# Keys of the quantised attention made beside the product keys; context splits and context loads moved

## Chip, cores and metric

The kernel runs on one core of a Trainium2 chip, in one launch. The metric is device time in microseconds, the median over several runs. It is float32 throughout, with matrix products split in high and low parts where exactness asks for it.

## What is computed

Four layers act on x (2, 512, 512), each a cross attention on a context of 2 x 1024 tokens (512 features) and a feed-forward part, each added through a gate. Layer 0 has a linear attention and a ternary feed-forward part; layer 1 a masked softmax attention and a product-key part; layer 2 a softmax attention whose queries, weights and outputs are quantised, and routed experts; layer 3 a plain softmax attention and routed experts beside a shared one. Cut to what the change touches:

```python
# layer 0 attention (16 heads of 32, 64 features per head)
q_prime = relu(einsum('bhnd,fd->bhnf', q, Wqf)); k_prime = relu(einsum('bhnd,fd->bhnf', k, Wkf))
kv = einsum('bhnf,bhne->bhfe', k_prime, v)
out = einsum('bhmf,bhfe->bhme', q_prime, kv) / (einsum('bhmf,bhf->bhm', q_prime, k_prime.sum(2))[..., None] + 1e-8)
# layer 1 feed-forward: 4 heads, 2 sides of 128 keys
q = (x @ Wq).reshape(b, t, H, 2, DK)
s1, i1 = top_k(einsum('bthd,hkd->bthk', q1, keys[:, :, 0]), 8)   # and s2, i2
final_scores, pk_idx = top_k(s1[..., :, None] + s2[..., None, :], 8)
# layer 2 attention: only the query side depends on x
q = qdq(x) @ qdq(wq).T + bq
k, v = split(ctx @ wkv.T + bkv, 2)
o = softmax(q k^T / sqrt(32)) v;   out = qdq(o) @ qdq(wp).T + bp
```

## The kernel before

Each stage of each layer is a block of hand-written programs, one per engine (TensorE, VectorE, ScalarE, GpSimd, and SyncE for transfers), joined by semaphores. An engine takes its instructions in the order in which they stand; so each queue's order is the schedule.

**Linear attention** (`linear_attention_block`, L2015). A hardware loop runs over FG = 4 groups of heads. In one pass ScalarE drains 12 products, `i` from 0 to 11: four for the keys (L2238), two for the queries (L2241), two guests (L2246) and four for the mapped queries (L2248), which TensorE makes at L2180 into two PSUM slots; then TensorE makes the outputs (L2188). As a side work each pass splits a quarter of the context into a high and a low part for the later layers, in four steps c: ScalarE copies the high part (L2196), GpSimd subtracts (L2264), ScalarE issues the store to `ctx_parts` (L2200). There is one slot for it, `part[:, 2]`, so the copy of a step waits until the store of the step before has landed. The splits stand ahead of i = 0, 3, 6, 9, and the stores behind i = 2, 5, 8, 11:

```python
if i % 3 == 0: split_context(f, i // 3)
...
if i % 3 == 2: store_context(f, i // 3)
```

**Product keys** (`product_keys_block`, L1120), inside the layer 1 feed-forward block. TensorE makes queries (L1159), then similarities for 8 token tiles (L1169, 8 matmuls of 256 columns a tile). For each tile ScalarE copies them out (L1199 to L1202) and, two tiles later, adds score pairs (L398 in `ffn_block`); GpSimd makes small sums (L1222 and around); VectorE takes the largest values (L1245 to L1271) and the routing masks of two tiles before (L411, L418 of `ffn_block`). GpSimd also makes one large subtraction for the feed-forward weights (L380) at tile 2. TensorE is done with the similarities early and then has nothing to do until the block ends.

**Softmax attention** (`streamed_attention_block`, L1375, with `ContextLoads` and `AttentionParts`). Heads are worked in 8 sets of two. Work comes in items. A key item K (there are 16, two a set) is 12 matmuls of 128x512 (4 context chunks, and three terms high-high, high-low, low-high, L1626), a high part on ScalarE (L1758), a low part on VectorE (L1869) and a 512 KB store to `k_parts` (L1530), from which SyncE loads stacks (L1549). Q items make queries (L1617), V items values (L1638), X, W and N quantise x and wq and normalise. An opening works a written list of items; then each set runs score matmuls (L1675), row maxima (L1654, L1893), exponentials (L1788), value products (L1689), and sums of the exponentials: GpSimd adds tiles of 128x2048 (L1859), `DIRECT[n]` of the 8 addends of a set go to TensorE instead, which folds all (L1709). In the two attentions without a mask DIRECT is 0 but for set 6, so seven additions a set for GpSimd and six in set 6. Items of later sets stand between the score matmuls. The opening of layer 2 waits for `biases_loaded`, three loads, of which that of `bv` is issued last (L1370), behind one key weight, half of the context, two value weights and wq.

**Routed experts** (`routed_block`, L915). For each of I = 23 slots of tokens GpSimd gathers rows (L1058), TensorE turns and multiplies them (L972 to L1004) and GpSimd scatters the sums (L1066). In layer 2's block SyncE also loads the weights and context of layer 3's attention, 11 issues of half a MB, all at once after 5 slots: `sp.wait_ge(y_done, I // 4)`; `ahead(sp)`.

## Time and profile before

| | us |
|---|---|
| median of 3 runs | 3107.15 (3104.47 to 3112.45) |
| profiled execution | 3111.91 |
| its span | 3110.2 |
| TensorE busy | 2633.1 (85%) |
| VectorE busy | 1759.4 (57%) |
| ScalarE busy | 1196.3 (38%) |
| GpSimd busy | 958.0 (31%) |
| mean granted TensorE clock | 0.917 |

The stages, by the timeline: linear attention to 348, ternary feed-forward to 575, masked attention to 960, norm and product keys to 1095, their feed-forward part to 1553, quantised attention to 2030, routed experts to 2250, plain attention to 2660, last feed-forward part to 3110. TensorE is busy nearly everywhere; VectorE has its share in the product keys, GpSimd in the three softmax attentions, and transfers peak at the openings. The granted clock is full in most slices and falls where TensorE rests.

### The profile page before, as it was taken

What the parts mean: (1) busy time and instruction counts of PE and PEld (TensorE: products, weight loads), DVE (VectorE), ACT (ScalarE), POOL (GpSimd) and SP (SyncE); (2) the same over time, 40 slices, a digit from 0 to 9 for tenths busy, and PEclk for the clock granted to TensorE, in tenths of its full rate; (3) what the DMA queues carried; (4) which work ended last, traced back from release to release, by engine and by line L of the source; (5) the groups of instructions that cost most, each with busy time, mean ns of one, the idle gap of its engine ahead of it and who ended that gap; (6) DMA issues with size and microseconds to landing.
All of it is one profiled execution on the core that took longest, in us unless ns stands there. A gap on an engine that the chain in (4) does not pass through costs nothing. (4 is left out here: it accounts for less than half of the span.)

```text
span 3110.2 us, 36063 instructions
## 1 busy us (share of the span) xinstructions
PE 2633.1 (85%) x11399; PEld 1679.8 (54%) x11399; DVE 1759.4 (57%) x3263; ACT 1196.3 (38%) x2550; POOL 958.0 (31%) x440
## 2 busy tenths in 40 slices
PE   7888699888887279999969998748789998699898
PEld 3455388655423156555556563325575653477555
DVE  2433477567765989899367674512266773444222
ACT  0222122266652688787014455211125554222111
POOL 0221000056633110010015886032217883222122
PEclk9898799899988589999989998869999998799999
DMA  9554113566400010100064541075365530211822
GB/s 275 190 195 172 58 72 106 148 177 176 126 1 31 1 54 28 55 27 27 14 212 125 155 124 44 1 271 131 75 187 142 153 104 1 81 42 52 273 58 46
DMA packets 136826, 327.21 MB, mean 105 GB/s; under 512 B 18400, under 2 KB 21472, under 8 KB 133344
## 3 DMA queue, kind: packets, MB, share of 16 engines
q1 hardware_dynamic: 109472, 256.41, 26.7%
q0 software_dynamic: 12864, 29.06, 4.0%
q10 hardware_dynamic: 14336, 39.85, 3.9%
q8 instruction: 77, 1.26, 0.2%
q14 instruction: 77, 0.63, 0.1%
HBM read 230.94 MB, written 97.72 MB: 106 GB/s over the span
## 5 line engine op out<-in xcount | busy, mean ns | idle before, releaser
L1859 POOL TENSOR_TENSOR L_attn_total<-L_attn_total,L_attn_probs 128x2048 f32<-128x2048 f32 x109 | 499.4, 4582 | 39.8 <-ACT L_attn_probs L1788 30.1
L1893 DVE TENSOR_REDUCE L_attn_row_max<-L_attn_rows_ps 128x1 f32<-128x512 f32 x512 | 340.1, 685 | 150.9 <-PE L_attn_rows_ps L1654 145.9
L1788 ACT ACTIVATE L_attn_probs<-L_attn_s_ps 128x512 f32<-128x512 f32 x512 | 289.7, 601 | 277.2 <-PE L_attn_s_ps L1675 274.5
L516 PE MATMUL L_ffn_hidden<-L_ffn_x_high,L_ffn_up_high 128*128 128x512 f32 x688 | 296.4, 431 | 100.5 <-DVE L_ffn_routes L432 54.9
L398 ACT ACTIVATE L_ffn_sums<-sims 128x128 f32<-128x128 f32 x1024 | 315.5, 389 | 47.7 <-DVE L_ffn_routes L418 26.6
L1675 PE MATMUL L_attn_s_ps<-L_attn_q_stack,L_attn_k_stack 98*128 98x512 f32 (+1 forms) x768 | 312.6, 433 | 22.3 <-ACT L_attn_probs L1788 20.5
L516 PE MATMUL L_ffn_hidden<-L_ffn_x_low,L_ffn_up_high 128*128 128x512 f32 x688 | 273.6, 398 | 0.0
L1675 PEld LDWEIGHTS L_attn_s_ps<-L_attn_q_stack,L_attn_k_stack 98*128 98x128 f32 (+1 forms) x768 | 145.7, 194 | 163.2 <-ACT L_attn_probs L1788 80.5
L537 PE MATMUL L_ffn_y<-L_ffn_down_in,L_ffn_h 128*128 128x512 f32 x512 | 229.1, 593 | 0.4 <-DVE L_ffn_h L644 0.4
L1654 PE MATMUL L_attn_rows_ps<-L_attn_k_stack,L_attn_q_stack 96*128 96x512 f32 x512 | 217.1, 427 | 14.3 <-DMA L_attn_k_stack<-k_parts 8.4
L1788 ACT ACTIVATE L_attn_probs<-L_attn_s_ps,keep_mask 128x512 f32<-128x512 f32 x256 | 183.8, 782 | 84.8 <-DVE L_attn_s_ps L1905 84.5
L516 PEld LDWEIGHTS L_ffn_hidden<-L_ffn_x_high,L_ffn_up_high 128*128 128x128 f32 x688 | 132.7, 193 | 151.8 <-issue 81.0
L1626 PE MATMUL L_attn_product_ps<-L_attn_ctx,L_attn_wk 128*128 128x512 f32 x576 | 172.5, 420 | 47.4 <-DVE L_attn_ones L1919 26.4
L380 POOL TENSOR_TENSOR L_ffn_up_low<-L_ffn_up_in,L_ffn_up_high 128x512 fp32r<-128x512 f32 (+1 forms) x30 | 66.6, 2224 | 456.4 <-ACT L_ffn_up_high L374 456.4
L1689 PE MATMUL L_attn_s_ps<-L_attn_probs,L_attn_values 128*32 128x512 f32 x1536 | 199.9, 631 | 1.5 <-ACT L_attn_probs L1788 1.4
L1905 DVE TENSOR_SCALAR L_attn_s_ps<-L_attn_s_ps 128x512 f32<-128x512 f32 x256 | 163.4, 688 | 60.5 <-PE L_attn_s_ps L1675 58.9
L1638 PE MATMUL L_attn_product_ps<-L_attn_wv,L_attn_ctx 128*128 128x256 f32 x1152 | 169.0, 288 | 14.4 <-DMA L_attn_wv<-L_attn_kv_parts 5.1
L1638 PEld LDWEIGHTS L_attn_product_ps<-L_attn_wv,L_attn_ctx 128*128 128x128 f32 x1152 | 163.5, 195 | 27.6 <-DVEq L1917 6.5
L516 PE MATMUL L_ffn_hidden<-L_ffn_x_high,L_ffn_up_low 128*128 128x512 f32 x432 | 173.2, 401 | 0.0
L1859 POOL TENSOR_TENSOR L_attn_total<-L_attn_probs 128x2048 f32<-128x2048 f32 x21 | 96.1, 4577 | 248.2 <-ACT L_attn_probs L1788 248.2
L1626 PEld LDWEIGHTS L_attn_product_ps<-L_attn_ctx,L_attn_wk 128*128 128x128 f32 x576 | 116.2, 203 | 77.6 <-DVE L_attn_ones L1919 27.7
L516 PEld LDWEIGHTS L_ffn_hidden<-L_ffn_x_low,L_ffn_up_high 128*128 128x128 f32 x688 | 133.2, 194 | 36.4 <-issue 10.5
(300 smaller groups left out, 4451.0 us busy)
## 6 DMA issues: line engine op xcount, KB each, us to landing
L_attn_k_stack<-k_parts SPq DMA_DIRECT2D x144, 256.0 KB, 4.8
k_parts<-L_attn_stage SPq DMA_DIRECT2D x48, 512.0 KB, 2.7
L_attn_q_stack<-q_parts SPq DMA_DIRECT2D x72, 256.0 KB, 6.3
L_attn_abs_in<-in_L_ffn_w SPq DMA_DIRECT2D x12, 1024.0 KB, 11.5
L_attn_kv_parts<-L_attn_part ACTq DMA_DIRECT2D x12, 1024.0 KB, 4.8
L_attn_wk<-L_attn_kv_parts SPq DMA_DIRECT2D x24, 512.0 KB, 4.3
L_attn_ctx<-ctx_parts SPq DMA_DIRECT2D x24, 512.0 KB, 10.9
L_attn_wv<-L_attn_kv_parts SPq DMA_DIRECT2D x24, 512.0 KB, 9.3
```

Source lines behind the costliest of these rows:

```text
L398: last = nc.scalar.activation(sums[:, h, a * NK:(a + 1) * NK], sims[:, t, h, KEY_ROWS:KEY_ROWS + NK], ACT.Identity, bias=sims[:, t, h, bas ...
L516: last = nc.tensor.matmul(hidden_ps[0:m, b, side, :], w[:, i, e0:e0 + m], x_parts[xp][:, i, h * HALF:(h + 1) * HALF], start=(q == 0), stop ...
L537: last = nc.tensor.matmul(y_ps[:, t % YB, :], h_parts[hp][0:m, s, c, t * P:(t + 1) * P], down_parts[wp][0:m, s, c, :], start=(q == 0), sto ...
L1626: last = nc.tensor.matmul(to, wk[:, w, c * P:(c + 1) * P], ctx[:, i, x, c, :], start=(c == 0 and (w, x) == TERMS[0]), stop=(c == DC - 1 an ...
L1638: last = nc.tensor.matmul(to[:, c // 2 * PAIR * P:(c // 2 + 1) * PAIR * P], ctx[:, i, x, d, at:at + P], wv[:, half, w, d % 2 * PAIR * P:(d ...
L1654: nc.tensor.matmul(rows_ps[:, r % R_SLOTS, :], q_stack[0:FOLD, n % Q_SLOTS, h, q * P:(q + 1) * P], k_stack[0:FOLD, n % 2, h, i * HALF:(i + ...
L1675: nc.tensor.matmul(s_ps[:, v % S_SLOTS, :], k_stack[0:depth, n % 2, h, kt * P:(kt + 1) * P], q_stack[0:depth, n % Q_SLOTS, h, :], start=Tr ...
L1689: last = nc.tensor.matmul(o_ps[HD * h:HD * (h + 1), :], values[:, n // PAIR % V_SLOTS, kt, at:at + HD], probs[:, g % P_SLOTS, h, :], start ...
L1788: nc.scalar.activation(probs[:, g % P_SLOTS, h, :], s_ps[:, v % S_SLOTS, :], ACT.Exp, **kinds).then_inc(exp_done, 1)
L1859: nc.gpsimd.tensor_tensor(total[:], first, probs[:, g % P_SLOTS], ALU.add).then_inc(added, 1)
L1893: nc.vector.tensor_reduce(row_max[:, hq, i:i + 1], rows_ps[:, r % R_SLOTS, :], AX_X, ALU.max, negate=True).then_inc(max_done, 1)
L1905: nc.vector.tensor_scalar(scores, scores, BOUND / SCALE, -BOUND / SCALE, ALU.min, ALU.max).then_inc(clipped, 1)
```

## The change

There are four parts, and the results are the same.

1. The 16 key items of layer 2's attention leave it. Their matmuls are in the product-key block, behind the similarities of tiles 2 to 7, by the table `AHEAD_AT`. A product goes into one of 4 PSUM slots that the queries used; ScalarE writes the high part and the raw product (L1226 and L1228 of the changed kernel) to one of 4 stage slots, GpSimd subtracts one from the other, SyncE stores 512 KB. The weights (4 x 512 KB) and the first of four context pieces (2 MB each, two buffers) are loaded in the norm block ahead. SyncE waits in the feed-forward block until the four slots are stored (`settle`), before the down weights are loaded.
2. Layer 2's attention has no K items. `bv` is loaded fourth, and the first key stacks before the second context half. The 32 row matmuls of set 0 ride on items V02 to Q11 rather than K10 to Q11. DIRECT is 1 for every set, so GpSimd makes six additions a set instead of seven, and TensorE folds one addend more.
3. Linear attention: splits at i = 1, 6, 8 and behind the loop's products; stores one product behind each, the last behind its split.
4. Layer 3's loads are ten pieces, issued at y_done of 1, 3, 5, ... 19, rather than all at 5.

```diff
 # product_keys_block
+    AHEAD_AT = {2: (0, 1), 3: (2, 3, 4), 4: (5, 6, 7), 5: (8, 9, 10), 6: (11, 12, 13), 7: (14, 15)}
 # SyncE
+                sp.wait_ge(q_psum, 2 * H)
+                ahead.load_piece(env, sp, 1)
+                for m in range(ahead.COUNT):
+                    ahead.store(env, sp, m)
+                    piece = m // DC + 2
+                    if m % DC == DC - 1 and piece < ahead.PIECES:
+                        sp.wait_ge(ahead.psum, m + 1)
+                        ahead.load_piece(env, sp, piece)
 # TensorE
+                def key_product(m):
...
+                    if m >= 4:
+                        pe.wait_ge(ahead.raw, m - 3)
+                    for c in range(DC):
+                        for w, x in TERMS:
+                            last = nc.tensor.matmul(q_ps[:, m % 4, :], ahead.wk[:, f, w, c * P:(c + 1) * P],
...
                 for t in range(2, TILES):
                     similarities(t)
+                    for m in AHEAD_AT[t]:
+                        key_product(m)
 # ScalarE
+                def key_parts(m):
...
+                    if m >= ahead.SLOTS:
+                        act.wait_ge(ahead.stored[s], 16 * (m // ahead.SLOTS))
+                    if m == 2:
+                        first["up_taken"](act)
+                    nc.scalar.activation(ahead.stage[s][:, 0], q_ps[:, m % 4, :], ACT.Identity, bias=bias).then_inc(
+                        ahead.high, 1)
+                    nc.scalar.activation(ahead.stage[s][:, 1].bitcast(F32), q_ps[:, m % 4, :], ACT.Identity,
+                                         bias=bias).then_inc(ahead.raw, 1)
 # GpSimd
+                def key_low(m):
...
+                    nc.gpsimd.tensor_tensor(stage[:, 1], stage[:, 1].bitcast(F32), stage[:, 0].bitcast(F32),
+                                            ALU.subtract).then_inc(ahead.low, 1)
 # streamed_attention_block
-    DIRECT = {n: int(n == SETS - 2) if less_max_rows else 3 if n == SETS - 2 else 2 for n in range(SETS - 1)}
+    made = parts.keys_made
+    DIRECT = {n: int(made or n == SETS - 2) if less_max_rows else 3 if n == SETS - 2 else 2 for n in range(SETS - 1)}
-        order = ("N0 K00 X0 X1 N2 V00 V01 X2 X3 W0 W1 N4 Q00 K01 X4 X5 W2 W3 N6 Q01 V02 V03 X6 X7 K10 K11 "
-                 "Q02 Q03 Q10 Q11 T0 Q12 Q13")
+        order = ("N0 X0 X1 N2 W0 W1 X2 X3 N4 Q00 V00 V01 X4 X5 W2 W3 N6 Q01 V02 V03 X6 X7 Q02 Q03 Q10 Q11 T0 Q12 Q13")
 # linear_attention_block
+    SPLIT_AT = {1: 0, K_PARTS + Q_PARTS: 1, K_PARTS + Q_PARTS + GUESTS: 2}
-                        if i % 3 == 0:
-                            split_context(f, i // 3)
+                        if i in SPLIT_AT:
+                            split_context(f, SPLIT_AT[i])
...
-                        if i % 3 == 2:
-                            store_context(f, i // 3)
+                        if i - 1 in SPLIT_AT:
+                            store_context(f, SPLIT_AT[i - 1])
...
+                    split_context(f, DC - 1)
+                    store_context(f, DC - 1)
 # routed_block
-                if ahead:
-                    sp.wait_ge(y_done, I // 4)
-                    ahead(sp)
+                pieces = ahead() if ahead else []
+                for k, piece in enumerate(pieces):
+                    sp.wait_ge(y_done, 1 + k * (I - 2) // len(pieces))
+                    piece(sp)
```

ScalarE, linear attention, from the drain of product 8 on (its own first row below is the drain, L2248; L2196 the context copy, L2200 its store, L2211 a split of later weights). Before:

```order
L2248 ACTIVATE L_attn_qf<-L_attn_proj_ps 128x512
L2199 REGISTER_ALU
L2200 ISA
L2200 DMA ctx_parts<-L_attn_part 256x1x512
L2195 ISA
L2196 ISA
L2196 COPY L_attn_part<-L_attn_ctxT 128x512
L2235 REGISTER_ALU
L2248 ACTIVATE L_attn_qf<-L_attn_proj_ps 128x512
```

and in the changed kernel (drain L2375, copy L2323, store L2327, later weights L2338):

```order
L2323 COPY L_attn_part<-L_attn_ctxT 128x512
L2362 REGISTER_ALU
L2375 ACTIVATE L_attn_qf<-L_attn_proj_ps 128x512
L2362 REGISTER_ALU
L2375 ACTIVATE L_attn_qf<-L_attn_proj_ps 128x512
L2326 REGISTER_ALU
L2327 ISA
L2327 DMA ctx_parts<-L_attn_part 256x1x512
L2336 REGISTER_ALU
L2337 REGISTER_ALU
L2338 CAST L_attn_part<-L_attn_later_raw 128x2x512
L2362 REGISTER_ALU
```

The copy that stood between the drains of products 8 and 9 stands ahead of that of 8; the next one stands behind the last drain of the pass.

SyncE, start of layer 2's attention, before:

```order
L1366 DMA L_attn_bq<-in_L_attn_bq 128x4
L1366 DMA L_attn_bk<-in_L_attn_bk 128x4
L1310 DMA L_attn_wk<-L_attn_kv_parts 128x1024
L1302 DMA L_attn_ctx<-ctx_parts 128x2x512 x4
L1314 DMA L_attn_wv<-L_attn_kv_parts 128x1024 x2
L1369 DMA L_attn_wq_raw<-wq_scratch 128x4x512
L1370 DMA L_attn_bv<-in_L_attn_bv 128x512
L1302 DMA L_attn_ctx<-ctx_parts 128x2x512 x4
```

and in the changed kernel (L1664 loads key stacks):

```order
L1473 DMA L_attn_bq<-in_L_attn_bq 128x4
L1473 DMA L_attn_bk<-in_L_attn_bk 128x4
L1475 DMA L_attn_wq_raw<-wq_scratch 128x4x512
L1476 DMA L_attn_bv<-in_L_attn_bv 128x512
L1370 DMA L_attn_wv<-L_attn_kv_parts 128x1024 x2
L1358 DMA L_attn_ctx<-ctx_parts 128x2x512 x4
L1664 DMA L_attn_k_stack<-k_parts 32x4x512 x6
L1358 DMA L_attn_ctx<-ctx_parts 128x2x512 x4
```

The load of `bv` stands behind 1 MB of wq rather than behind that and seven half-MB loads.

ScalarE, product keys, from the pair sums of the third tile on (L398; L1199 or L1244 copies similarities), before:

```order
L398 ACTIVATE L_ffn_sums<-sims 128x128 x16
L374 CAST L_ffn_up_high<-L_ffn_up_in 128x2048
L1199 COPY L_ffn_full<-L_ffn_sims_ps 128x1024
L1201 COPY sims<-L_ffn_full 128x4x32
L1202 COPY sims<-L_ffn_full 128x4x128
L398 ACTIVATE L_ffn_sums<-sims 128x128 x16
```

and in the changed kernel (names of the slots differ, `L_ffn_up_in` is one of them):

```order
L398 ACTIVATE L_ffn_sums<-sims 128x128 x16
L374 CAST L_ffn_up_high<-L_ffn_up_in 128x2048
L1226 ACTIVATE ahead_stage<-L_ffn_q_ps,ahead_bk 128x512
L1228 ACTIVATE ahead_stage<-L_ffn_q_ps,ahead_bk 128x512
L1226 ACTIVATE ahead_stage<-L_ffn_q_ps,ahead_bk 128x512
L1228 ACTIVATE ahead_stage<-L_ffn_q_ps,ahead_bk 128x512
L1244 COPY L_ffn_full<-L_ffn_sims_ps 128x1024
L1246 COPY sims<-L_ffn_full 128x4x32
L1247 COPY sims<-L_ffn_full 128x4x128
L398 ACTIVATE L_ffn_sums<-sims 128x128 x16
L1226 ACTIVATE L_ffn_up_in<-L_ffn_q_ps,ahead_bk 128x512
L1228 ACTIVATE L_ffn_up_in<-L_ffn_q_ps,ahead_bk 128x512
```

Between two tiles stand two or three pairs of activations on key products.

## Rows read from the trace of the kernel before

**Rows 1.** Timeline, linear attention: start, us, operation, idle before and its releaser.
```profile
130.22 1.22 PE L2180 MATMUL L_attn_proj_ps<-L_attn_qT,L_attn_wqf 128*128 128x512 f32 x1 [7.12 <-ACT L_attn_qf L2248]
...
189.87 0.62 ACT L2196 CAST L_attn_part<-L_attn_ctxT 128x512 fp32r x1 [5.80 <-DMA ctx_parts<-L_attn_part]
...
191.04 1.22 PE L2180 MATMUL L_attn_proj_ps<-L_attn_qT,L_attn_wqf 128*128 128x512 f32 x1 [5.79 <-ACT L_attn_qf L2248]
...
307.93 0.70 PE L2180 MATMUL L_attn_proj_ps<-L_attn_qT,L_attn_wqf 128*128 128x512 f32 x1 [2.78 <-ACT L_attn_qf L2248]
```

**Rows 2.** Timeline, TensorE, then VectorE over one tile of the product keys.
```profile
996.78 1.89 PE L1169 MATMUL L_ffn_sims_ps<-L_ffn_keys,L_ffn_qT 128*128 128x256 f32 x8
...
1060.97 1.64 DVE L1245 MAX8 L_ffn_best<-L_ffn_full 128x8 f32<-128x128 f32 x8
...
1067.63 0.75 DVE L411 SCALAR_TENSOR_TENSOR L_ffn_sums<-L_ffn_sums,bar 128x512 f32<-128x512 f32 x1
...
1071.63 0.29 DVE L1245 MAX8 L_ffn_best<-L_ffn_full 128x8 f32<-128x128 f32 x1
```

**Rows 3.** Windows, that tile: us, busy of PE, PEld, DVE, ACT, POOL, PEclk, DMA.
```profile
1060.97:1071.63 10.66, 0.00 (x0) 0.00 (x0) 9.97 (x37) 6.70 (x21) 1.05 (x4) 0.50 0.00 1
```

**Rows 4.** Timeline, one GpSimd operation and the VectorE operation that began under it.
```profile
1020.87 4.52 POOL L380 TENSOR_TENSOR L_ffn_up_low<-L_ffn_up_in,L_ffn_up_high 128x2048 fp32r<-128x2048 f32 x1 [3.75 <-ACT L_ffn_up_high L374]
...
1020.90 5.04 DVE L411 SCALAR_TENSOR_TENSOR L_ffn_sums<-L_ffn_sums,bar 128x512 f32<-128x512 f32 x1
```

**Rows 5.** Timeline, TensorE and ScalarE, prices in the quantised attention.
```profile
1616.72 0.86 PE L1626 MATMUL L_attn_product_ps<-L_attn_ctx,L_attn_wk 128*128 128x512 f32 x3
...
1617.42 0.40 PE L1654 MATMUL L_attn_rows_ps<-L_attn_k_stack,L_attn_q_stack 96*128 96x512 f32 x1
...
1749.11 0.68 ACT L1758 ACTIVATE L_attn_stage<-L_attn_product_ps,L_attn_bk 128x512 fp32r<-128x512 f32 x1
...
1890.98 0.63 PE L1654 MATMUL L_attn_rows_ps<-L_attn_k_stack,L_attn_q_stack 96*128 96x512 f32 x1
...
1891.41 0.63 PE L1675 MATMUL L_attn_s_ps<-L_attn_q_stack,L_attn_k_stack 98*128 98x512 f32 x1
```

**Rows 6.** The page, DMA issues: KB each, us from issue to landing.
```profile
k_parts<-L_attn_stage SPq DMA_DIRECT2D x48, 512.0 KB, 2.7
```

**Rows 7.** Timeline, start of the quantised attention's opening.
```profile
1561.93 1.03 SPq L1370 DMA_DIRECT2D L_attn_bv<-in_L_attn_bv  x1
...
1573.43 0.30 ACT L1802 ACTIVATE L_attn_sd<-tile_meanvar,eps_ln 128x8 f32<-128x8 f32 x1 [11.91 <-DMA L_attn_bv<-in_L_attn_bv]
```

**Rows 8.** Windows, that opening, columns as before.
```profile
1573.40:1652.80 79.40, 64.44 (x302) 52.21 (x302) 64.44 (x105) 14.41 (x26) 5.43 (x4) 0.89 0.60 177
```

**Rows 9.** Timeline, GpSimd and TensorE, the sets of the quantised attention.
```profile
1721.79 0.80 PE L1654 MATMUL L_attn_rows_ps<-L_attn_k_stack,L_attn_q_stack 96*128 96x512 f32 x1 [4.39 <-DMA L_attn_k_stack<-k_parts]
...
1778.58 4.59 POOL L1859 TENSOR_TENSOR L_attn_total<-L_attn_probs 128x2048 f32<-128x2048 f32 x1 [2.26 <-ACT L_attn_probs L1788]
...
1793.19 1.29 POOL L1838 TENSOR_TENSOR L_attn_heads<-L_attn_spare 128x512 f32<-128x512 f32 x1
...
1887.67 1.93 PE L1709 MATMUL L_attn_product_ps<-L_attn_total,L_attn_ones 128*32 128x512 f32 x8 [2.02 <-POOL L_attn_total L1859]
```

**Rows 10.** Windows, sets 0 to 5 together, set 4 alone, set 6 alone.
```profile
1660.14:1891.04 230.90, 222.77 (x1232) 140.02 (x1232) 161.57 (x249) 119.93 (x216) 198.78 (x47) 0.98 0.48 131
1815.52:1853.01 37.49, 36.91 (x211) 23.56 (x210) 27.52 (x43) 19.98 (x37) 33.33 (x8) 1.00 0.41 106
1891.04:1925.95 34.91, 29.70 (x128) 11.51 (x126) 14.83 (x23) 17.52 (x33) 28.48 (x7) 0.79 0.00 1
```

**Rows 11.** Timeline, routed experts: the last load of a burst, and a wait.
```profile
2122.60 5.49 SPq L1302 DMA_DIRECT2D L_attn_ctx<-ctx_parts  x4
...
2129.97 0.47 PE L972 MATMUL L_ffn_x_ps<-ident,L_ffn_xg 128*128 128x128 f32 x1 [8.05 <-DMA L_ffn_xg<-L_ffn_x_slots]
```

More of the change, by code:

```diff
@@ L1212, in _ @@
             def _(pool):
+                def key_low(m):
+                    stage = ahead.stage[m % ahead.SLOTS]
+                    pool.wait_ge(ahead.high, m + 1)
+                    pool.wait_ge(ahead.raw, m + 1)
+                    nc.gpsimd.tensor_tensor(stage[:, 1], stage[:, 1].bitcast(F32), stage[:, 0].bitcast(F32),
+                                            ALU.subtract).then_inc(ahead.low, 1)
                 for t in range(TILES):
@@ L1223, in _ @@
                         first["gpsimd"](pool)
+                    for m in AHEAD_AT.get(t, ()):
+                        key_low(m)
             @block.vector
@@ L1320, in load_first, with pieces_ahead @@
         self.load_value_weights(sp, 0)
+    def pieces_ahead(self, env):
+        self.ahead = True
+        halves = [[lambda sp, i=i, c=c: self.load_context(env, sp, 0, i, c) for c in range(DC)] for i in range(CTX // HALF)]
+        return [lambda sp: self.load_key_weights(sp, 0), *halves[0], lambda sp: self.load_value_weights(sp, 0), *halves[1]]
     def load_ahead(self, env, sp):
@@ L1325, in load_ahead, with __init__, place, load_weights @@
         self.load_half(env, sp, 0, 1)
+class KeysAhead:
+    PIECES, SLOTS = BATCH * CTX // HALF, 4
+    def __init__(self, env, kv_parts, bias):
+        env.prefix = "L2_keys_ahead"
+        self.kv_parts, self.bias = kv_parts, bias
+        self.weights_loaded = env.sem("weights_loaded")
+        self.ctx_loaded = [env.sem(f"ctx_loaded{s}") for s in range(2)]
+        self.psum, self.high, self.raw, self.low = env.sem("psum"), env.sem("high"), env.sem("raw"), env.sem("low")
+        self.stored = [env.sem(f"stored{s}") for s in range(self.SLOTS)]
+        self.COUNT = self.PIECES * DC
+    def place(self, env, first, stage_at, ctx_at, local):
+        nc = env.nc
+        self.wk = local.enter_context(nc.sbuf_tensor("ahead_wk", [P, DC, 2, DC * P], F32R))
+        self.bk = local.enter_context(nc.sbuf_tensor("ahead_bk", [P, DC], F32))
+        early = nc.alloc_sbuf_tensor_at("ahead_stage", [P, 2, 2, HALF], F32R, offset=stage_at)
+        late = first["up_in"].rearrange("p (s h n) -> p s h n", s=2, h=2).bitcast(F32R)
+        self.stage = [early[:, 0], early[:, 1], late[:, 0], late[:, 1]]
+        second = nc.alloc_sbuf_tensor_at("ahead_ctx", [P, 2, DC, HALF], F32R, offset=ctx_at)
+        self.ctx = [[up.rearrange("p (c n) -> p c n", c=DC) for up in first["up_next"]], [second[:, 0], second[:, 1]]]
+    def load_weights(self, sp):
+        sp.dma_start(self.bk[:], self.bias).then_inc(self.weights_loaded, 16)
+        for f in range(DC):
+            sp.dma_start(self.wk[:, f].bitcast(F32), self.kv_parts[f, :, 0].bitcast(F32)).then_inc(self.weights_loaded, 16)
+    def load_piece(self, env, sp, piece):
+        for part in range(2):
+            sp.dma_start(self.ctx[piece % 2][part].bitcast(F32), env.ctx_parts[piece, :, part].bitcast(F32)).then_inc(
+                self.ctx_loaded[piece % 2], 16)
+    def store(self, env, sp, m):
+        piece, f = m // DC, m % DC
+        halves = CTX // HALF
+        sp.wait_ge(self.low, m + 1)
+        sp.dma_start(env.k_parts[piece // halves * DC + f, piece % halves].bitcast(F32),
+                     self.stage[m % self.SLOTS].bitcast(F32)).then_inc(self.stored[m % self.SLOTS], 16)
+    def settle(self, sp):
+        for s in range(self.SLOTS):
+            sp.wait_ge(self.stored[s], 16 * (self.COUNT // self.SLOTS))
@@ L1398, in streamed_attention_block @@
     CHUNK_AT = {u: (item, c) for item, units in enumerate(((0, 1, 3, 4), (8, 9, 11, 12), (14, 15, 16, 17), (20, 21, 23, 24)))
-                for c, u in enumerate(units)}
-    DONE_AT = {max(u for u in CHUNK_AT if CHUNK_AT[u][0] == i) + 1: i for i in range(4)}
+                for c, u in enumerate(units) if not made or item % 2 == 0}
+    DONE_AT = {max(u for u in CHUNK_AT if CHUNK_AT[u][0] == i) + 1: i for i in range(0, 4, 1 + made)}
     SUMS_AT = 7 if less_max_rows else PV_AT
@@ L1544, in stack_keys @@
                 def stack_keys(n, i):
-                    stored(sp, ("K", n, i))
+                    if not made:
+                        stored(sp, ("K", n, i))
                     if n >= 2:
@@ L1568, in _ @@
                 ready = []
+                if made:
+                    loads.load_value_weights(sp, 0)
+                    loads.load_half(env, sp, 0, 0)
+                    for i in range(KH):
+                        stack_keys(0, i)
+                    loads.load_half(env, sp, 0, 1)
                 for item in OPENING:
@@ L2611, in attention_layer @@
                         key_mask_block(env, name, keep_mask)
-                    parts = AttentionParts(env, name, loads, work)
+                    parts = AttentionParts(env, name, loads, work, kinds.get("keys_made", False))
                     streamed_attention_block(env, name, heads_out, parts, keep_mask, env.io["wo"], early, quantised)
```

88 lines of the change are left out of this document (63 added, 25 removed).

## The prediction

> **What bounds the kernel now.** I read first the page's busy slices, to see which engine limits which stage, then the timeline of each stage that the change touches, for the waits that end last there, and then windows over one period of each, for how much room the other engines have.
>
> In the **linear attention** the chain runs through ScalarE's drains. The second mapped product waits for a PSUM slot: 7.12 us of idle TensorE in the first pass, 5.79 in the second, 2.78 in the last (the third, not shown, like the second). Just ahead of each the copy of a context chunk has stood 5.80 us for the store before it, and it takes 0.62 itself [rows 1]. So a side work's landing is on the path, four times.
>
> In the **product keys** VectorE is the bound: one tile takes from 1060.97 to 1071.63, 10.66 us [rows 2], of which VectorE is busy 9.97, ScalarE 6.70, GpSimd 1.05 and TensorE not at all, at a granted clock of 0.50, the lower level [rows 3].
>
> In the **quantised attention** the opening loses 11.91 us to the load of `bv`, issued at 1561.93 behind all others [rows 7], and from there to the first scores at 1652.8 TensorE and VectorE are each busy 64.4 of 79.4 us [rows 8]. In the sets both TensorE and GpSimd are near their limit: TensorE 222.8 of 230.9 us over six sets, and of set 4's 37.49 us GpSimd 33.3, TensorE 36.9 [rows 10].
>
> In the **routed experts** SyncE issues the last four of 11 loads at 2122.60, and TensorE then stands 8.05 us for gathered rows [rows 11].
>
> **The sum**, against the profiled execution of 3111.9 us, which is 4.8 above the median of the runs shown.
>
> *Linear attention: -24.* The copy leaves the place between products 8 and 9. Waits of TensorE there are 7.12 + 5.79 + 5.79 + 2.78 = 21.5, and four copies of 0.62 add 2.5 to the chain [rows 1]. In their new places, the copy at i = 8 falls in the time in which ScalarE waits for TensorE's key maps, that at i = 1 waits for the last of the pass before, issued under the outputs; the last stands behind all drains. None adds to the chain unless a store lands later than there. Low end -27 (the clock of the last matmuls gains too), high end -15, if a third of it comes back as a wait at another step.
>
> *Product keys: +12.* Added to each of tiles 3 to 6: 36 matmuls on TensorE, six activations on ScalarE, three subtractions on GpSimd (tiles 2 and 7: two thirds). TensorE: 36 x 0.233 (three of this shape from 1616.72 to 1617.42 [rows 5]) is 8.4, and the 8 similarities 1.9 [rows 2], so 10.3 against 10.66: just hidden, since the engine is idle there. ScalarE: 6.70 + 6 x 0.68 [rows 3, 5] = 10.8: also about even, and tiles 2 and 7 have fewer. GpSimd: three of 1.29 [rows 9] are room enough. But its operations hit VectorE. While GpSimd held one of 4.52 us, a VectorE operation that began 0.03 us later took 5.04 [rows 4] and not its usual 0.75 [rows 2]. So the bound engine pays for each of 16 subtractions: 0 if none meets an operation of two inputs, and 16 x 1.29 = 20.6 if each is paid in full. Operations of that sort are the seven masks and routes of a tile (L411, L418), at 0.75 each [rows 2] some 5 us, and the small ones at L1265 to L1267, some 1.3: about 0.6 of the tile, so 16 x 1.29 x 0.6 = 12 is taken. The Trainium skill, SBUF — State Buffer, "SBUF: two separate sides", says that the port pair that the two share is an exclusive lock held for a whole instruction; by it each collision costs the rest of GpSimd's operation, and the part would be 20 rather than 12 if VectorE always needed the lock. The row of 5.04 us agrees. The loads (10 MB with the weights) run where the transfers stand still [rows 3]. The ring of four slots: product 2.8, two activations 1.4, subtraction 1.3, store 2.7 [rows 5, 6, 9], about 8 to 12 us around, against 3.5 us an item: that is 14 us for four, so it doesn't bind. `settle` finds the last store a few us old; the down weights behind it are needed only after the first up products.
>
> *Opening: -20.* `bv` lands before it is needed, -11 (11.91 less what is left of a shorter queue). Four key items leave the 79.4 us: 48 matmuls x 0.233 = 11.2 us of TensorE and four parts of 0.7 on VectorE; with TensorE 81% busy I take -9. Ends: -14 (items move into gaps) and -24.
>
> *Sets: -22.* A set loses one GpSimd addition (4.59), 24 matmuls (5.6) on TensorE, and gets 8 short ones (0.9). GpSimd's cycle would be 37.5 - 4.6 = 32.9, TensorE's 36.9 - 4.7 = 32.2. Against that, the one set with six additions and no key items, set 6, took 34.91 with a clock of 0.79 [rows 10], because TensorE waits for GpSimd at the fold (2.02 us) [rows 9] and then runs at the lower level: 0.43 us from 1890.98 to 1891.41 [rows 5]. I take 34.9 for each of the six: 6 x 34.9 = 209.4, against 230.9, which also holds the 4.39 us in which a key stack was late [rows 9]. Ends: -33 (6 x 32.9) and -5 (only the stall goes).
>
> *Loads of layer 3: -6* of the 8.05 us [rows 11], since one piece at a time lets the gathers through; ends 0 and -10. Everything behind is as before.
>
> Sum: -24 + 12 - 20 - 22 - 6 = **-60**: the profiled execution would be 3052, the median **3047**.
>
> **Rivals.**
>
> *A. TensorE stays at the lower level in the product keys.* It stood at 0.50 there [rows 3], and a wait between products could hold it. Then 36 x 0.43 + 3.8 = 19.3 us a tile for four tiles and 14.1 for two: 4 x 8.6 + 2 x 3.5 = +42 and not +12, so 3077. Against: with 97% of the tile filled it never rests.
>
> *B. Collisions in full and no gain from spreading.* +20.6 for +12, 0 for -6: 3062. The Trainium skill, DMA: Bandwidth & Descriptors, "Queues, rings and completion order", says that each engine takes packets from its queues in turn; spread loads would then still halve the gathers as they pass, only at ten places. The row at 2129.97 can't tell a burst from a stream.
>
> *C. The sets keep their cycle.* Set 6's clock says how: with less work TensorE rests, slows, and scores come at the old pace. Only the stall goes: -5 for -22, so 3064.
>
> *D. Slower: the slot ring.* If a round of PSUM, ScalarE, GpSimd and store takes R, each item takes R/4, and ScalarE, waiting for `stored`, holds back the similarity copies and pair sums that VectorE lives on. The six tiles take 64 us; the change turns slower where 16 R / 4 is over 64 + 12 + 60 - that is R above 34. With 40: 160 - 64 = +96 for +12, 3131. For it: ScalarE is at 10.8 of 10.7, and GpSimd queues behind VectorE in the same collisions. Against: four stages of 8 us.
>
> *E. The change does not do what it says*: GpSimd's one addition less and the keys' absence are undone by waits on values and queries, so that the time stays within 0.3% (9 us, about what a measurement of this kernel tells from no change).
>
> **How the numbers follow.** The forecast has 0.62, A 0.12, B 0.09, C 0.12, D 0.03, E 0.02. The best ends together give -27 + 0 - 24 - 33 - 10 = -94, the worst -15 + 20.6 - 14 - 5 - 0 = -13. The range leaves the tails, D and E, out: 3020 to 3080, which holds A, B and C. Faster 0.95, same 0.02, slower 0.03.
>
> **What would show it.** In the linear attention no TensorE wait at the mapped products over 1 us, and 24 us less at its end. In the product keys TensorE at full clock at tiles 3 to 6 with a period of about 12.5 us on VectorE, some of its operations above 1.5 us; a period of 19 with a pitch of 0.43 is A, activations waiting for `stored` are D. In the opening no wait for `bv` and the first score 20 us sooner. In the sets a period near 35 and PEclk of 0.8 to 0.9; near 33 is better than forecast, near 37 is C. In the routed experts no wait of 8 us for gathered rows. The forecast is wrong if VectorE waits for ScalarE in the product keys, or if a wait for key stacks comes up in the sets.

## The result, and the profile after

| | us |
|---|---|
| before, median | 3105.81 (3103.9 to 3112.45) |
| changed, median | 3058.24 (3056.32 to 3059.69) |
| ratio | 0.9843, 95% interval 0.9826 to 0.986 |
| changed, profiled execution, span | 3057.55, 3055.8 |
| TensorE, VectorE, ScalarE, GpSimd busy | 2624.9, 1756.1, 1205.2, 951.3 |
| mean granted TensorE clock | 0.933 |

The change is faster by 48 us. Between the two profiled executions it is 54.4. Anchors that both traces have, such as the first turn behind the linear attention or the first matmul of a stage, put these 54.4 us in their places:

| part | forecast | between the traces |
|---|---|---|
| linear attention | -24 | -27.0 (turn at 325.04, now 298.04) |
| up to the queries of the product keys | 0 | -2.2 (976.93, now 947.77) |
| product keys | +12 | +12.1 (118.3 to 130.4 from first query to first hidden product) |
| opening of layer 2 | -20 | -10.9 (98.1 to 87.2 from the first load to the first score) |
| sets 0 to 5 | -22 | -13.5 (230.9 to 217.4) |
| routed experts | -6 | -9.3 (244.1 to 234.8 from the first turn to the first product of layer 3) |
| all else | 0 | -3.6 |

**Linear attention.** In the timeline of the changed kernel (start, duration, operation, idle before and its releaser) the copy of the third split still waits for the store before it, but now ahead of the drain of product 8, where ScalarE has nothing to drain before 173.26; and TensorE goes from the mapped products to the outputs with a short wait only:

```profile
161.01 0.62 ACT L2323 CAST L_attn_part<-L_attn_ctxT 128x512 fp32r x1 [3.81 <-DMA ctx_parts<-L_attn_part]
...
177.33 1.10 PE L2315 MATMUL L_attn_o_ps<-L_attn_kv,L_attn_qf 128*128 128x66 f32 x8 [1.43 <-ACT L_attn_qf L2375]
...
231.10 1.10 PE L2315 MATMUL L_attn_o_ps<-L_attn_kv,L_attn_qf 128*128 128x66 f32 x8 [1.44 <-ACT L_attn_qf L2375]
```

The pass is 52.6 us from 124.78 to 177.33, where it was about 60; nothing answers to the waits of 7.12, 5.79 and 2.78 us [rows 1]. Two windows over the whole loop, before and changed (us, busy of PE, PEld, DVE, ACT, POOL, PEclk, DMA share, GB/s):

```profile
78.00:325.04 247.04, 204.71 (x774) 125.56 (x772) 103.25 (x237) 49.88 (x76) 48.34 (x28) 0.87 0.54 186
...
78.00:298.04 220.04, 195.16 (x773) 119.79 (x771) 99.50 (x237) 49.89 (x76) 48.34 (x28) 0.92 0.58 206
```

Of the 27.0 us, 17.5 are idle time of TensorE (42.3 to 24.9) and 9.5 are busy time: the same matmuls run at a granted clock of 0.92 instead of 0.87.

**Product keys.** One tile on VectorE, with the operation at L1321 (0.87 us in a tile of the kernel before, where it is L1265), and below it GpSimd's two rows of subtractions in that tile:

```profile
1040.18 1.64 DVE L1301 MAX8 L_ffn_best<-L_ffn_full 128x8 f32<-128x128 f32 x8
...
1044.67 2.81 DVE L1321 SCALAR_TENSOR_TENSOR L_ffn_reach<-L_ffn_pairs,bar 128x64 f32<-128x64 f32 x4
...
1053.21 0.28 DVE L1301 MAX8 L_ffn_best<-L_ffn_full 128x8 f32<-128x128 f32 x1
```

```profile
1043.23 1.29 POOL L1264 TENSOR_TENSOR L_ffn_up_in<-L_ffn_up_in 128x512 fp32r<-128x512 f32 x1 [0.23 <-ACT L_ffn_up_in L1228]
...
1044.48 2.53 POOL L1264 TENSOR_TENSOR ahead_stage<-ahead_stage 128x512 fp32r<-128x512 f32 x2
```

The tile takes 13.03 us and was 10.66 [rows 2]. The subtractions lie from 1043.23 to 1047.01. VectorE's four small operations at L1321 begin under the second one and take 2.81 us, 1.94 more; another 0.36 is a longer gap ahead of L1305. The seven masks and routes have their usual times, since GpSimd is done when they begin. The window over the tile, in the columns above:

```profile
1040.18:1053.21 13.03, 5.45 (x23) 3.84 (x21) 11.98 (x37) 10.16 (x27) 4.82 (x7) 0.86 0.31 122
```

ScalarE is at 10.16, and TensorE's clock 0.86 rather than 0.50 [rows 3]. (Some of its matmul records are missing there.) The waits listed for ScalarE in these tiles are for VectorE's masks, none for a store of the ring.

**Opening.** ScalarE's first operation waits 0.33 us for `bv` and not 11.91 [rows 7]; but TensorE stands 4.46 us for a row maximum that VectorE can only take behind its last normalisation:

```profile
1545.27 0.30 ACT L1927 ACTIVATE L_attn_sd<-tile_meanvar,eps_ln 128x8 f32<-128x8 f32 x1 [0.33 <-DMA L_attn_bv<-in_L_attn_bv]
...
1586.45 1.39 PE L1779 MATMUL L_attn_rows_ps<-L_attn_k_stack,L_attn_q_stack 96*128 96x512 f32 x2 [4.46 <-DVE L_attn_row_max L2019]
```

The window from the first normalisation to the first score is 80.0 us, as long as before (79.4), though TensorE's work fell from 64.4 to 57.0 [rows 8]. VectorE's fell by 2.3.

```profile
1545.27:1625.28 80.01, 56.98 (x266) 46.26 (x266) 62.16 (x101) 11.97 (x22) 5.37 (x4) 0.79 0.63 181
```

**Sets.** A set is 32 units of one score and one row matmul each; a value or key item is laid between them in four pieces, the chunks. The windows are sets 0 to 5 together, then sets 1, 3 and 5, and 4 us within set 3:

```profile
1632.65:1850.01 217.36, 207.02 (x1137) 114.39 (x1136) 152.39 (x237) 112.87 (x205) 170.84 (x42) 0.98 0.39 98
...
1667.95:1703.92 35.97, 34.12 (x195) 18.88 (x193) 25.95 (x41) 18.94 (x35) 28.69 (x7) 1.00 0.65 183
...
1741.37:1778.75 37.38, 35.52 (x194) 20.14 (x193) 25.91 (x41) 18.75 (x35) 28.64 (x8) 0.95 0.37 93
...
1816.15:1850.01 33.86, 31.93 (x171) 15.82 (x169) 25.12 (x40) 18.50 (x35) 28.69 (x8) 1.00 0.33 87
...
1749.00:1753.00 4.00, 4.00 (x19) 3.61 (x18) 1.73 (x3) 1.19 (x2) 3.86 (x2) 0.57 0.53 131
```

GpSimd's busy time in the six sets fell from 198.8 to 170.8, TensorE's from 222.8 to 207.0 [rows 10], yet set 3 takes 37.4 us where it took 36.9. Within it the clock is 0.57 from 1749 to 1753. Rows of TensorE, the first from set 1, the others from set 3 up to that drop:

```profile
1674.78 0.50 PE L1779 MATMUL L_attn_rows_ps<-L_attn_k_stack,L_attn_q_stack 96*128 96x512 f32 x1 [0.98 <-DVE L_attn_row_max L2019]
...
1746.49 0.50 PE L1779 MATMUL L_attn_rows_ps<-L_attn_k_stack,L_attn_q_stack 96*128 96x512 f32 x1 [0.50 <-DVE L_attn_row_max L2019]
...
1748.19 0.50 PE L1779 MATMUL L_attn_rows_ps<-L_attn_k_stack,L_attn_q_stack 96*128 96x512 f32 x1 [0.96 <-DVE L_attn_row_max L2019]
...
1749.59 0.63 PE L1779 MATMUL L_attn_rows_ps<-L_attn_k_stack,L_attn_q_stack 96*128 96x512 f32 x1
...
1750.02 1.48 PE L1763 MATMUL L_attn_product_ps<-L_attn_wv,L_attn_ctx 128*128 128x256 f32 x6
```

Units without a chunk come one after the other here; each has a score and a row matmul, 0.47 us, and a maximum of 0.685 us on VectorE, for which there are two PSUM slots. TensorE waits 0.50 and 0.96 us for a maximum, and then a row matmul takes 0.63 and six value matmuls 1.48 rather than 0.87 us: the lower level. But the wait does not settle it: sets 1 and 5 have the same waits (0.48 and 0.98) and stay at 1.00, while sets 2, 3 and 4 fall to 0.95 each. That difference costs 1.4 us (36.0 against 37.4), and what decides it is not shown.

The trace of before shows little of this. The list of waits (us in total, times, longest), over sets 2 to 4 before and then in the changed kernel, has:

```profile
PEld L_attn_rows_ps L1654 <- DVE L_attn_row_max L1893: 4.7, 12, 0.5
...
PEld L_attn_rows_ps L1779 <- DVE L_attn_row_max L2019: 19.1, 36, 1.4
PE L_attn_rows_ps L1779 <- DVE L_attn_row_max L2019: 4.9, 9, 1.0
```

Before, no matmul of these three sets is listed as waiting for a maximum, only 12 weight loads.

**Routed experts.** SyncE's loads come over some 120 us (four of them from 2058.32 in the first row), and the longest wait for gathered rows in that time is one of 3.10 us, against 8.05 [rows 11]:

```profile
2058.32 40.85 SPq L1358 DMA_DIRECT2D L_attn_ctx<-ctx_parts  x4
...
2126.39 0.66 PE L978 MATMUL L_ffn_x_ps<-ident,L_ffn_xg 128*128 128x128 f32 x4 [1.09 <-DMA L_ffn_xg<-L_ffn_x_slots]
...
2154.84 0.66 PE L978 MATMUL L_ffn_x_ps<-ident,L_ffn_xg 128*128 128x128 f32 x4 [3.10 <-DMA L_ffn_xg<-L_ffn_x_slots]
```

### The profile page after: what moved, and what is told of

The parts are those of the page before. It is cut to its first block and busy times, and to the rows that moved or that the text cites. A ratio compares the mean times of both kernels' runs of the same rounds, so it can differ in the third digit from the quotient of the medians.

```text
span 3055.8 us, 36190 instructions
## 1 busy us (share of the span) xinstructions
PE 2624.9 (86%) x11447; PEld 1668.5 (55%) x11447; DVE 1756.1 (57%) x3247; ACT 1205.2 (39%) x2566; POOL 951.3 (31%) x450
## 5 line engine op out<-in xcount | busy, mean ns | idle before, releaser
L1985 POOL TENSOR_TENSOR L_attn_total<-L_attn_total,L_attn_probs 128x2048 f32<-128x2048 f32 x103 | 471.5, 4577 | 29.7 <-ACT L_attn_probs L1913 19.7
L398 ACT ACTIVATE L_ffn_sums<-sims 128x128 f32<-128x128 f32 x1024 | 315.4, 389 | 41.2 <-DVE L_ffn_routes L418 25.8
L1779 PE MATMUL L_attn_rows_ps<-L_attn_k_stack,L_attn_q_stack 96*128 96x512 f32 x512 | 223.4, 440 | 24.4 <-DVE L_attn_row_max L2019 17.6
L1779 PEld LDWEIGHTS L_attn_rows_ps<-L_attn_k_stack,L_attn_q_stack 96*128 96x128 f32 x512 | 99.2, 194 | 90.4 <-DVE L_attn_row_max L2019 71.7
L542 PEld LDWEIGHTS L_ffn_y<-L_ffn_down_in,L_ffn_h 128*128 128x128 f32 x512 | 93.5, 191 | 98.9 <-issue 98.9
```

Source lines behind the costliest of these rows:

```text
L398: last = nc.scalar.activation(sums[:, h, a * NK:(a + 1) * NK], sims[:, t, h, KEY_ROWS:KEY_ROWS + NK], ACT.Identity, bias=sims[:, t, h, bas ...
L542: last = nc.tensor.matmul(y_ps[:, t % YB, :], h_parts[hp][0:m, s, c, t * P:(t + 1) * P], down_parts[wp][0:m, s, c, :], start=(q == 0), sto ...
L1779: nc.tensor.matmul(rows_ps[:, r % R_SLOTS, :], q_stack[0:FOLD, n % Q_SLOTS, h, q * P:(q + 1) * P], k_stack[0:FOLD, n % 2, h, i * HALF:(i + ...
L1985: nc.gpsimd.tensor_tensor(total[:], first, probs[:, g % P_SLOTS], ALU.add).then_inc(added, 1)
```

## The experiments

All are measured beside runs of the kernel before on the same chip; a kernel's runs lie within 3 to 19 us of each other, so that the place of a difference is read from the profiled execution and its sign from the interval.

**The subtractions.** The changed kernel without `key_low`, so that the low parts of these keys stay the raw products:

```diff
-                    nc.gpsimd.tensor_tensor(stage[:, 1], stage[:, 1].bitcast(F32), stage[:, 0].bitcast(F32),
-                                            ALU.subtract).then_inc(ahead.low, 1)
...
-        sp.wait_ge(self.low, m + 1)
+        sp.wait_ge(self.high, m + 1)
+        sp.wait_ge(self.raw, m + 1)
```

> The changed kernel without the 16 subtractions of GpSimd in the product keys; the low part of the early keys is left as the raw product, so the keys of layer 2 are not the reference's. Theory (a GpSimd operation on 128x512 holds back VectorE by about 0.8 us each, and nothing else lengthened a tile): the period of a tile on VectorE goes from 13.05 us in the changed kernel back to 10.7, and the kernel from 3058 to about 3046, -12. Rival (ScalarE's six more activations of 0.68 us a tile lengthen it, since similarity copies and pair sums stand behind them): the period stays at 13 and the time at 3058.

Measured: 3053.2 us, ratio 0.9828 (0.9806 to 0.985); the profiled execution 3048.3. A tile on VectorE, and the window over it:

```profile
1023.35 1.64 DVE L1292 MAX8 L_ffn_best<-L_ffn_full 128x8 f32<-128x128 f32 x8
...
1033.95 1.64 DVE L1292 MAX8 L_ffn_best<-L_ffn_full 128x8 f32<-128x128 f32 x8
```

```profile
1023.35:1033.95 10.60, 10.60 (x49) 8.86 (x48) 9.92 (x36) 10.18 (x27) 1.05 (x4) 1.00 0.65 263
```

The period is 10.60 us, and the stage 118.8 us, against 130.4 with the subtractions and 118.3 before. ScalarE's 10.18 us fit into the tile, and TensorE is busy all of it at full clock. So 16 subtractions cost 11.6 us, 0.73 each, and 192 matmuls, 32 activations, the transfers and the slots cost 0.5, no more than the stage varies between runs of one code (130.4 to 131.6). The rival falls. The whole kernel gained less than the stage, 5 us in the medians and 9.3 in the profiled executions: sets 1 and 5 have the drop of the clock in this execution (37.4 and 35.3 us for 36.0 and 33.9), which takes back 2.9.

**The order of the value chunks.** In layer 2 only:

```diff
-    CHUNK_AT = {u: (item, c) for item, units in enumerate(((0, 1, 3, 4), (8, 9, 11, 12), (14, 15, 16, 17), (20, 21, 23, 24)))
+    CHUNK_AT = {u: (item, c) for item, units in enumerate(((0, 2, 4, 6), (), (9, 13, 17, 21), ()) if made else
```

> The changed kernel with the two value items of a set at units 0, 2, 4, 6 and 9, 13, 17, 21 instead of 0, 1, 3, 4 and 14, 15, 16, 17, in layer 2 alone. Theory (row maxima on VectorE, 0.685 us each, pace the units that carry no product chunk, and TensorE rests there, drops to the lower clock level and loses the rest): the wait of about 1 us and the stretch at half clock behind it go, the period of sets 2 to 4 falls from 37.4 to about 35, and the six periods together from 217 to about 205, so 3046. Rival (GpSimd or ScalarE sets the cycle, or the clock drops whatever the order): within 3 us of 3058.

Measured: 3059.8 us, ratio 0.9846 (0.9823 to 0.9868), no different from the change, as the rival had it. Sets 2 to 4 take 35.9 us each; set 3, and a wait in set 1:

```profile
1743.79:1779.69 35.90, 34.40 (x194) 19.11 (x193) 25.54 (x41) 18.31 (x35) 28.64 (x7) 1.00 0.38 97
...
1688.08 0.50 PE L1780 MATMUL L_attn_rows_ps<-L_attn_k_stack,L_attn_q_stack 96*128 96x512 f32 x1 [2.28 <-DMA L_attn_k_stack<-k_parts]
```

The clock is 1.00 in sets 2 to 5, and the waits of 0.5 and 1.0 us are gone there, so the drop of the clock is a matter of where the chunkless units stand, worth 1.5 us a set. But 35.9 is also what set 1 of the changed kernel took at full clock (36.0): beyond the clock the new places gave nothing. Set 1 takes 38.8 for 36.0, with a wait of 2.28 us for a key stack and a clock of 0.96, which took 2.8 back: the six sets are 215.2 us for 217.4, not 205. The theory holds for the clock alone.

**Seven additions.**

```diff
-    DIRECT = {n: int(made or n == SETS - 2) if less_max_rows else 3 if n == SETS - 2 else 2 for n in range(SETS - 1)}
+    DIRECT = {n: int(n == SETS - 2) if less_max_rows else 3 if n == SETS - 2 else 2 for n in range(SETS - 1)}
```

> The changed kernel with DIRECT as before: seven additions on GpSimd in sets 0 to 5, and eight matmuls fewer on TensorE at the fold. Theory (VectorE and TensorE pace a set, GpSimd has 6.8 us of waiting in each): a set gets 0 to 1 us shorter or stays, 3052 to 3060. Rival (GpSimd's additions set the cycle, so that the sixth addition's removal is where the gain of the sets comes from): a set gets up to 4.6 us longer where GpSimd's wait was smaller, 3065 to 3080.

Measured: 3068.8 us, ratio 0.9882 (0.9858 to 0.9906). Sets 2 and 5:

```profile
1703.55:1741.15 37.60, 34.75 (x186) 20.01 (x185) 25.92 (x41) 18.93 (x35) 33.26 (x8) 0.95 0.36 92
...
1816.32:1855.00 38.68, 33.77 (x162) 17.28 (x161) 24.95 (x40) 18.43 (x34) 33.16 (x9) 0.90 0.29 76
```

Sets 2 to 4 take 37.6 us, 0.2 more than with six additions. TensorE has eight matmuls fewer, 0.9 us, and waits 0.97 us at each fold for GpSimd: the one pays for the other. Set 5, whose window has one value item instead of two, goes from 33.9 to 38.7: there GpSimd, busy 33.2 us, is the bound again. So the removed addition paid 4.8 us in one set and 1.3 in the other five together, at the pace that VectorE sets. A set of 32.9 us, as in the run with short maxima below, would have no room for 33.3 us of additions.

**Rows behind the last normalisation.**

```diff
-        order = ("... N6 Q01 V02 V03 X6 X7 Q02 Q03 Q10 Q11 T0 Q12 Q13")
+        order = ("... N6 Q01 X6 X7 V02 V03 Q02 Q03 Q10 Q11 T0 Q12 Q13")
```

> The changed kernel with X6 and X7 ahead of V02 and V03 in the opening of layer 2, so that no row matmul waits for VectorE's last normalisation. Theory (the opening is a chain on VectorE: normalisations, then 32 row maxima of set 0; TensorE's 4.46 us of waiting and its half clock behind it are covered): the first score moves by 3 us at most, 3055 to 3060. Rival (that wait and the lower clock that follows cost what the key items' removal should have saved): 3050 or less.

Measured: 3064.7 us, ratio 0.9871 (0.9844 to 0.9897), the profiled execution 3054.4; the interval overlaps that of the change. From the first normalisation to the first score it takes 81.5 us, for 80.0. The wait of 4.46 us is gone and nothing is won: it was covered. Set 1:

```profile
1668.70:1706.12 37.42, 35.53 (x194) 20.20 (x193) 25.95 (x41) 18.96 (x35) 28.67 (x8) 0.95 0.63 176
```

It had 36.0 in the changed kernel, and set 5 takes 35.3 for 33.9: whether a set has the drop of the clock can differ where its code is the same.

**Half of each maximum.** Maxima over 256 of 512 scores:

```diff
-                    nc.vector.tensor_reduce(row_max[:, hq, i:i + 1], rows_ps[:, r % R_SLOTS, :], AX_X, ALU.max,
+                    wide = SEQ // 2 if made else SEQ
+                    nc.vector.tensor_reduce(row_max[:, hq, i:i + 1], rows_ps[:, r % R_SLOTS, 0:wide], AX_X, ALU.max,
```

> The changed kernel with the row maxima of layer 2 taken over 256 of each 512 scores, so that VectorE's reduction is about half as long (some 0.4 instead of 0.685 us). The other half of the scores is left out of the maximum that is subtracted before the exponential, nothing else. Theory (VectorE's maxima pace the units without a product chunk, and the second half of the opening): sets 2 to 4 fall from 37.4 us to 32 to 34 each, no wait of TensorE for a maximum remains, and the time from the first normalisation to the first score falls from 80 us by 6 to 10; in all 3058 to about 3030. Rival (GpSimd's additions or ScalarE's exponentials set the period): sets within 1 us of 37.4, opening unchanged, 3053 to 3060.

Measured: 3037.9 us, ratio 0.9766 (0.975 to 0.9782). One maximum, then the windows of set 2 and of the opening:

```profile
1730.02 0.36 DVE L2020 TENSOR_REDUCE L_attn_row_max<-L_attn_rows_ps 128x1 f32<-128x256 f32 x1
```

```profile
1695.86:1728.78 32.92, 32.20 (x194) 18.93 (x193) 18.08 (x40) 18.18 (x35) 28.75 (x7) 1.00 0.43 106
...
1547.16:1623.16 76.00, 54.09 (x265) 45.35 (x266) 52.37 (x101) 11.97 (x22) 5.38 (x4) 0.81 0.67 190
```

Sets 1 to 4 take 32.9 us each, with TensorE busy 32.2: 4.5 less than sets 2 to 4 had, of which 1.4 is the clock, and 3.1 less than set 1, which had been at full clock. That is the 32.2 that the prediction had worked out for TensorE; the rest is one wait of 0.7 us a set for a maximum, which the expectation had as gone. GpSimd still waits 3.6 us in each. VectorE's maxima are what held the sets. In the opening 10 us less work on VectorE gave 4.0, less than the 6 to 10 expected: VectorE is not alone in that chain. This kernel is the fastest here, 20 us below the change. It subtracts a number that need not be the row's maximum, which is exact in exact arithmetic and safe while the other half's scores are not higher by more than an exponential can hold.

**The matmuls put back.** Row matmuls issued four times where key chunks stood:

```diff
-                            row(of, r)
+                            row(of, r, 4 if made and n + AHEAD < SETS and u in (8, 9, 11, 12, 20, 21, 23, 24) else 1)
```

> The changed kernel with the row matmul issued four times instead of once at units 8, 9, 11, 12, 20, 21, 23, 24 of sets 0 to 5 of layer 2, where the key chunks stood; 24 matmuls a set are added, 5.6 us of TensorE, as many as the change took out. Theory (the key chunks stood in time that TensorE has to wait for VectorE anyway, and kept its clock up): the periods of sets 2 to 4 stay at 36.5 to 38, 3055 to 3065. Rival (TensorE's own work sets the period and 5.6 us less of it was a gain given back elsewhere): each set gets 4 to 5.6 us longer, 3080 or more.

Measured: 3073.0 us, ratio 0.9872 (0.9846 to 0.9899). Set 3:

```profile
1748.64:1787.64 39.00, 38.22 (x219) 23.80 (x218) 26.26 (x41) 18.97 (x35) 28.77 (x8) 1.00 0.36 89
```

A set takes 39.0 us: 1.6 more than the changed kernel's 37.4, and 3.0 more than a set of it at full clock (set 1, 36.0). The clock is 1.00. Neither expectation holds: of 5.6 us of matmuls 2.6 are hidden behind VectorE, and 1.4 come back as clock, so that in sets 2 to 4 TensorE's relief was worth 1.6 us and not 5.6. A repeated row matmul also delays its own maximum, which a key chunk did not; the 1.6 is thus an upper end.

**The splits alone**, on the kernel before (GpSimd's subtractions follow them; not shown):

```diff
-                        if i % 3 == 0:
-                            split_context(f, i // 3)
+                        if i in SPLIT_AT:
+                            split_context(f, SPLIT_AT[i])
...
-                        if i % 3 == 2:
-                            store_context(f, i // 3)
+                        if i - 1 in SPLIT_AT:
+                            store_context(f, SPLIT_AT[i - 1])
```

> The kernel before with the context splits of the linear attention moved, alone. Theory (each pass has one landing of a store and one copy between products 8 and 9 on the chain): -27 us, as between the two traces at the end of the linear attention, 3079 against 3106. Rival (part of the 27 comes from elsewhere, as the transfers of the changed norm block): less than 22.

Measured: 3084.0 us, ratio 0.9917 (0.989 to 0.9945). The first turn is at 298.24 against 325.04 before, -26.8, and the span 3082.3, -27.9. The loop to that turn:

```profile
78.00:298.24 220.24, 195.31 (x774) 119.58 (x772) 99.48 (x237) 49.85 (x76) 48.36 (x28) 0.92 0.58 206
```

The whole gain is the splits', that of the clock too.

**`bv` first alone**, on the kernel before (its later load goes):

```diff
+        if self.early_bias:
+            sp.dma_start(self.bv[:], io["bv"].partition_broadcast(P)).then_inc(self.biases_loaded, 16)
         if not self.loads.ahead:
             self.loads.load_first(env, sp)
```

> The kernel before with the load of bv in layer 2 ahead of the key weight, the context and the value weights, alone; the keys stay where they are. Theory (the opening gained only by the earlier load, the key items' removal nothing): the first normalisation starts some 12 us sooner but TensorE's first key item still waits for its context, 16 us after the block's start, so that X0 and what is behind it on TensorE stand behind it: -6 to -11. Rival (VectorE's chain is held by the key item ahead of X0 and X1 on TensorE): under 3 us of gain.

Measured: 3100.1 us, ratio 0.9974 (0.9959 to 0.9989). From the first load to the first score 91.8 us, for 98.1: -6.3. The new wait, on TensorE and, behind it, on VectorE:

```profile
1565.15 5.05 PE L1630 MATMUL L_attn_product_ps<-L_attn_ctx,L_attn_wk 128*128 128x512 f32 x12 [16.99 <-DMA L_attn_ctx<-ctx_parts]
...
1571.10 0.75 DVE L1873 SCALAR_TENSOR_TENSOR L_attn_stage<-L_attn_product_ps,L_attn_bk,L_attn_stage 128x512 fp32r<-128x512 f32 x1 [6.71 <-ACT L_attn_stage L1762]
```

The first key item still stands 16.99 us for its context, and VectorE, long done with the first normalisation, 6.71 us for that item. Of the change's 10.9 us the earlier bias alone gives 6.3. The other 4.6 come with the key items' absence and the new order of loads and items, which were not tested apart; VectorE's wait in this place is 2.00 us in the changed kernel, 4.7 less.

**The spread loads alone**, on the kernel before:

```diff
-                if ahead:
-                    sp.wait_ge(y_done, I // 4)
-                    ahead(sp)
+                pieces = ahead() if ahead else []
+                for k, piece in enumerate(pieces):
+                    sp.wait_ge(y_done, 1 + k * (I - 2) // len(pieces))
+                    piece(sp)
```

> The kernel before with the loads of layer 3's attention spread over the routed experts, alone. Theory (a burst of 5.5 MB held one gather back by 8 us, single pieces hold none back): -9 us, as between the traces. Rival (each engine takes packets from its queues in turn, so that spread loads slow ten gathers a little): within 3 us.

Measured: 3098.0 us, ratio 0.9967 (0.995 to 0.9985). From the first turn to layer 3's first product 231.2 us, for 244.1: -12.9, and -9.3 in the changed kernel. The windows from the first gathered rows to that product, before and here:

```profile
2074.43:2259.60 185.17, 145.53 (x598) 104.83 (x598) 45.34 (x155) 30.05 (x71) 48.96 (x44) 0.91 0.43 108
...
2072.29:2243.21 170.92, 139.71 (x599) 100.19 (x599) 45.19 (x155) 29.97 (x71) 49.01 (x44) 0.95 0.46 112
```

Of 14.3 us in them 8.4 are TensorE's idle time and 5.8 its busy time, at 0.95 for 0.91. No wait for gathered rows is over 1.79 us here, and the kernel before has some of up to 1.94 after its burst, when nothing is loaded: the pieces cost nothing that can be told from a gather's own time.

## Why the prediction was right, and where it was off

The forecast was 3047 us, 60 below, with 3020 to 3080; it came out at 3058, 48 below. Sign, range and the list of parts hold; the sizes of the parts do so less, and they err both ways. Of E nothing is left, and D's ring never bound: no activation waits for a store, and in the run without subtractions the tile was 10.60 us with 32 activations and all stores in it.

*Linear attention, -24.* The mechanism is that of the step, and alone it gave 26.8: the waits moved to a place where ScalarE stood idle, 3.81 us in the row above. That the sum came so near is partly luck. It took 21.5 us of waits and 2.5 of copies, but TensorE's wait up to 191.04 already holds the copy from 189.87 on [rows 1], so the copies were counted twice; and some 4 us of waits came back, 1.44 us ahead of the outputs for 0.86, and one of 0.46 behind them, in each pass. TensorE's idle time fell by 17.5 and not by 24. The missing 9.5 us are the clock, which the step had at its low end only, as 3 us in the last matmuls.

*Product keys, +12.* The number is right (12.1), and the cause: 11.6 of it is the subtractions. The working behind the 12 is right only in part. It took masks and routes as the ones that are hit; in the tile read above they are not. GpSimd's place in the tile, behind VectorE's best values, lays the second and third subtraction of a tile over the small operations at L1321, which grew by 1.94 us; that 0.73 a piece agrees with 0.6 x 1.29 is partly luck. The Trainium skill, SBUF — State Buffer, "SBUF: two separate sides", has a VectorE operation with two SBUF inputs and a GpSimd operation that reads SBUF lock each other out. The trace agrees: the four at L1321, with two inputs, take 2.81 us for 0.87, and four MAX8, with one, take 0.61 under the first subtraction, for 0.67 before. Paid in full the subtractions would have been 20 us. Rival A did not come: TensorE was at full clock in the run without subtractions, and at 0.86 with them, with no time lost by it that the tile shows.

*Opening, -20.* The first half, -11 for `bv`, looks right by the row (0.33 for 11.91), but it is not to be had alone: alone it is worth 6.3, because a key item with a late context stood behind it. The failed step is the second, "-9": with TensorE 81% busy, 11.2 us of its work were taken to be worth 9. From the first normalisation to the first score it takes 79.4 us before, 85.0 with the bias early and the keys kept, 80.0 in the change: the second half is worth 5, and how much of that is the keys' absence is open. Maxima of half the length gave 4.0; a TensorE wait of 4.46 gone gave nothing. The opening hands over from one engine to the other, and what is busy most is not what is waited for.

*Sets, -22.* The term was mis-sized: 13.5. Its engines were TensorE (32.2) and GpSimd (32.9). TensorE's number is borne out by the run with short maxima; that this run's period is 32.9 says nothing for GpSimd's, which waits 3.6 us in it. What failed is that VectorE, busy 27.5 of 37.5 us [rows 10], is not in the sum. Its maxima are one per unit, with two slots, and it can make up nothing where units without chunks follow each other. Key chunks had filled just those, and so the trace of before hardly showed it. The row that the step gave for set 6's clock, 2.02 us at 1887.67 [rows 9], is the fold at the end of set 5. Rival C was the nearer one for sets 2 to 4 (37.4), and in part by the mechanism that it names, TensorE slower after a rest: that is 1.4 us, and the rest was a wait for VectorE, not for want of work. Of the 13.5 us, 7.5 are set 1 (43.5 to 36.0), 4.2 set 5, 2.7 set 0, and the three in the middle lost 0.8. Set 1's stall was 4.39 us [rows 9], but the set was 6.5 longer than its neighbours, at a clock of 0.92 against their 1.00; the forecast had counted the stall alone.

*Loads, -6.* Right in kind, and low: 9.3 and 12.9. The step counted the wait and not the clock, 5.8 us in the run with this part alone. The Trainium skill, DMA: Bandwidth & Descriptors, "Queues, rings and completion order", has engines taking packets from queues in turn, and rival B made a loss of it. No run here shows that loss: the changed kernel has one wait of 3.10 us at a piece, and the run with this part alone none over 1.79.

The sum was 60 where the parts gave 54 between traces, and 48 between medians. The rest of that difference is the profiled execution of before, 6 us above its median.
